# Four gate and up tiles of the FFN made before the attention's last projections, and a new order of loads within a chunk

## The reference, cut to what matters

```python
# B, S, D = 4, 512, 512; 32 heads of 16; FFN width 1376 (padded to 11 tiles of 128)
x = x + attention(layernorm(x))      # qkv with bias, causal, ALiBi bias in the scores, softmax, w_proj, b_proj
h = layernorm(x)
x = x + (silu(h @ w_gate.T) * (h @ w_up.T)) @ w_down.T
```

## Time and profile before

| | |
|---|---|
| median of 3 runs | 911.36 us (910.64 to 912.17) |
| the profiled execution: its time, its span | 909.81 us, 908.1 us |
| TensorE busy (matmuls) | 843.0 us, 93% |
| VectorE busy | 468.9 us, 52% |
| ScalarE busy | 358.1 us, 39% |
| GpSimd busy | 187.8 us, 21% |
| TensorE's mean granted clock | 0.98 of full |
| moved by DMA | 109.33 MB, mean 120 GB/s |

### The profile page before, as it was taken

One profiled execution on the slowest core, in us unless ns is written; L12 is line 12 of the kernel. 1 busy time (PEld: TensorE's weight loads), 2 busy tenths in 40 slices (PEclk: granted clock), 3 DMA queues, 4 the chain that ended last, 5 costly groups with the idle time before them and its releaser, 6 DMA issues. The chain is left out here.

```text
span 908.1 us, 13759 instructions
## 1 busy us (share of the span) xinstructions
PE 843.0 (93%) x5088; PEld 597.8 (66%) x5088; DVE 468.9 (52%) x931; ACT 358.1 (39%) x693; POOL 187.8 (21%) x337
## 2 busy tenths in 40 slices
PE   1998799999999999999998489999999999999998
PEld 1755465656566565656654268887888788878886
DVE  7486766767777676767772353443122322231233
...
GB/s 261 184 238 118 155 133 186 184 137 180 172 222 157 135 179 197 230 128 159 167 200 81 71 298 108 70 1 139 1 1 1 138 1 0 0 94 45 0 0 46
DMA packets 70562, 109.33 MB, mean 120 GB/s; under 512 B 13395, under 2 KB 38662, under 8 KB 70505
## 3 DMA queue, kind: packets, MB, share of 16 engines
...
## 5 line engine op out<-in xcount | busy, mean ns | idle before, releaser
L839 DVE TENSOR_REDUCE bm<-bank 128x3 f32<-128x384 f32 (+1 forms) x384 | 217.5, 593 | 108.2 <-PE bank L1045 107.5
L700 ACT ACTIVATE pt<-bank 128x512 f32<-128x512 f32 (+1 forms) x384 | 196.8, 529 | 175.5 <-PE bank L1067 163.2
L1043 PE MATMUL bank<-k_st,q_st 97*128 97x512 bf16 (+3 forms) x512 | 143.8, 307 | 12.7 <-DMA q_st<-slopes_dram 10.3
L1332 DVE TENSOR_TENSOR gu<-bank,silu 128x512 f32<-128x512 f32 x44 | 30.5, 692 | 219.9 <-issue 130.6
L1143 PE MATMUL bank<-fT_hi,wgu_hi 128*128 128x512 f32 x352 | 138.8, 394 | 5.5 <-DVE wgu_lo L1304 3.5
L1067 PE MATMUL bank<-q_st,k_st 116*128 116x512 bf16 (+3 forms) x512 | 133.1, 303 | 7.3 <-ACT pt L700 6.0
L1143 PE MATMUL bank<-fT_lo,wgu_hi 128*128 128x512 f32 x352 | 138.3, 393 | 0.0
L1143 PE MATMUL bank<-fT_hi,wgu_lo 128*128 128x512 f32 x352 | 137.7, 391 | 0.0
L1045 PE MATMUL bank<-mask_qk,identb 128*128 128x128 bf16 x512 | 107.0, 221 | 0.0
L1043 PEld LDWEIGHTS bank<-k_st,q_st 97*128 97x128 bf16 x512 | 47.4, 98 | 67.9 <-issue 35.6
L1275 ACT ACTIVATE silu<-bank 128x512 f32<-128x512 f32 x44 | 26.3, 598 | 158.2 <-PE bank L1143 158.2
...
## 6 DMA issues: line engine op xcount, KB each, us to landing
...
```

The lines of the kernel that those rows point to most:

```text
L700: act.activation(pt[:, h % PT_RING, COL0[k]:COL0[k] + WIDE[k]], bank[3 + (3 * h + k) % 2][:, 0:WIDE[k]], ACT.Exp, scale=1.0 / HD).then_inc ...
L839: dve.tensor_reduce(bm[:, h % 4, BM_AT[k]:BM_AT[k] + BM_N[k]], bank[k][:, 0:BM_N[k] * P].rearrange("p (n q) -> p n q", q=P), AX.X, ALU.max ...
L1043: pe.matmul(bank[k][:, at:at + n], q_st[0:K_MAX, s, h % 4, t * P:(t + 1) * P], k_st[0:K_MAX, s, h % 4, 0:n], start=True, stop=False)
L1332: dve.tensor_tensor(gu[:, f % 2, :], bank[5 + 2 * (f % 2)][:, :], silu[:, f % 2, :], ALU.mult).then_inc(gu_done, 1)
```

## The change

- Weights: `w_hi` and `w_lo` are now held for the whole program. The attention uses them for w_qkv; from chunk 28 on, when the last q, k, v tile is made, they take the split gate and up weights of FFN tiles 0 to 3 (`EARLY = 4`) and four slots of gated values.
- These weights are loaded in chunks 26 (into the scratch of the parts) and 28 (into `xt`), cast by ScalarE in chunks 28 and 29, split by VectorE in chunks 29 and 30. In chunk 31 the raw weights of tiles 4 and 5 are loaded into `xt`.
- Behind the last weighing TensorE makes tile 0, projection block 2, tiles 1 and 2, block 3, tile 3, for the first batch. ScalarE and VectorE gate them (`gate`, `high`, `gated`).
- In the FFN's first batch `gate_up` runs over tiles 4 to 10; down tiles follow by `DOWN_BEHIND`, down weights are loaded and split on semaphores of their own.
- SyncE: in each chunk the stacks' loads come ahead of the group's load; the store of inverses ahead of Q parts; the store of token tile 2 one chunk later.
- TensorE: token transposes stand behind the weighing (step (0, 1)) and at step (1, 2); the transpose of the maxima one step later.
- ScalarE: copies of transposed tokens behind the head's third exponential; K's second part ahead of it. GpSimd: K's third part ahead of the masks; bias of tile 2 one head later. VectorE: the read of projection tile 2 in the next chunk; the inversion of row sums ahead of the head's last maxima.

```diff
+        w_hi = whole.enter_context(nc.sbuf_tensor("w_hi", [P, KT * 3 * D], F32R))
+        w_lo = whole.enter_context(nc.sbuf_tensor("w_lo", [P, KT * 3 * D], F32R))
+        n = EARLY * 2 * KT * P
+        wgu_e_hi, wgu_e_lo = [w[:, 0:n].rearrange("p (f c k m) -> p f c k m", f=EARLY, c=2, k=KT) for w in (w_hi, w_lo)]
+        gu_hi, gu_lo = [w[:, n:n + EARLY * S].rearrange("p (f s) -> p f s", f=EARLY) for w in (w_hi, w_lo)]
...
+        scratch = sb("scratch", [P, 4 * S])
+        part = scratch[:, 0:3 * S].bitcast(BF16).rearrange("p (c a s) -> p c a s", c=2, a=3)
+        rest = scratch[:, 3 * S:4 * S]
+        wgu_raw = [scratch[:, 2 * S * f:2 * S * (f + 1)].rearrange("p (c k m) -> p c k m", c=2, k=KT) for f in range(2)]
+        wgu_raw += wgu_early
+        silu = scratch[:, 0:2 * S].rearrange("p (f s) -> p f s", f=2)
+        gu = scratch[:, 2 * S:4 * S].rearrange("p (f s) -> p f s", f=2)
...
@@ -532,13 +560,13 @@
             store_parts("Q", 0, 2)
             for c in range(CHUNKS):
                 b, cb = c // CB, c % CB
-                if cb in (1, 3, 7) and loaded_at(c) is not None:
-                    load_group(loaded_at(c))
                 if c + 3 < CHUNKS and cb != 5:
                     load_stacks(c + 3)
                 if cb == 3 and b > 0:
                     load_residual(b - 1, 2)
                     store_tokens(b - 1, 1)
+                if cb in (1, 3, 7) and loaded_at(c) is not None:
+                    load_group(loaded_at(c))
...
                 if cb == 4 and b > 0:
+                    store_tokens(b - 1, 2)
                     store_tokens(b - 1, 3)
                 if cb == 4 and b + 2 <= B:
                     load_tokens(b + 2)
-                if cb == 4 and b == B - 1:
+                if c == CHUNKS - 6:
+                    for s in parts_stored:
+                        sp.wait_ge(s, GROUPS * PARTS_INCS)
+                    for f in range(2):
+                        sp.dma_start(wgu_raw[f], wgu_d[f]).then_inc(raw_in[f], 16)
+                if c == CHUNKS - 4:
                     sp.wait_ge(tile_done, tiles_done("T", B, KT - 1))
+                    for f in range(2, EARLY):
+                        sp.dma_start(wgu_raw[f], wgu_d[f]).then_inc(raw_in[f], 16)
+                if c == CHUNKS - 1:
                     for i in range(2):
-                        sp.dma_start(wgu_early[i], wgu_d[i]).then_inc(early_in[i], 16)
+                        sp.wait_ge(early_lo_done, 2 * (i + 3))
+                        sp.dma_start(wgu_early[i], wgu_d[EARLY + i]).then_inc(early_in[i], 16)
                 if cb == 5:
                     load_group(loaded_at(c))
+                if sums_of(c) is not None:
+                    store_inverses(sums_of(c))
...
-                if cb in (2, 3) and b > 0:
-                    store_tokens(b - 1, 2 * (cb - 2))
-                if sums_of(c) is not None:
-                    store_inverses(sums_of(c))
+                if cb == 2 and b > 0:
+                    store_tokens(b - 1, 0)
...
@@ -637,16 +675,16 @@
                         for kind, mb, g in made(c)[:1]:
                             if kind == "Q":
                                 third_part(kind, mb, g)
-                    clear_future(4 * c + i)
                     if i == 0:
                         for kind, mb, g in made(c - 1)[1:]:
                             if kind == "K":
                                 third_part(kind, mb, g)
+                    clear_future(4 * c + i)
                     if i == 3 and statistics_at(c) is not None:
                         reciprocal_deviation(statistics_at(c))
                     if b > 0 and cb == 1 and i in (0, 2):
                         add_bias(b - 1, i // 2)
-                    if b > 0 and (cb, i) == (3, 2):
+                    if b > 0 and (cb, i) == (3, 3):
...
+            def weight_hi(f, c):
+                act.wait_ge(raw_in[f], 16)
+                act.copy(wgu_e_hi[:, f, c, :, :], wgu_raw[f][:, c, :, :]).then_inc(early_hi_done, 1)
+
+            def gate(f):
+                act.wait_ge(gate_done, f + 1)
+                act.wait_ge(early_lo_done, 2 * EARLY)
+                need(act, gu_done, f - 1)
+                act.activation(silu[:, f % 2, :], bank[GATE_BANK[f % 2]][:, :], ACT.Silu).then_inc(silu_done, 1)
+
+            def high(f):
+                act.wait_ge(gu_done, f + 1)
+                act.copy(gu_hi[:, f, :], gu[:, f % 2, :]).then_inc(gu_hi_done, 1)
...
                     exponential(h, 0)
-                    if tokens_at(c, i) is not None and i == 0:
-                        transposed_hi(*tokens_at(c, i))
                     if i == 3:
                         for tile in made(c)[:1]:
                             if tile[0] == "Q":
                                 second_part(*tile)
                     exponential(h, 1)
-                    if tokens_at(c, i) is not None and i == 1:
-                        transposed_hi(*tokens_at(c, i))
+                    if i == 0:
+                        for tile in made(c - 1)[1:]:
+                            if tile[0] == "K":
+                                second_part(*tile)
                     if highs(c, i) is not None:
                         attention_hi(*highs(c, i))
                     exponential(h, 2)
+                    if tokens_at(c, i) is not None:
+                        transposed_hi(*tokens_at(c, i))
...
+                    if c in (CHUNKS - 4, CHUNKS - 3):
+                        weight_hi(2 * (c - CHUNKS + 4) + i // 2, i % 2)
             attention_hi(*highs(CHUNKS, 0))
             copy_pv(CHUNKS - 1)
+            gate(0)
+            high(0)
             for i in range(HALVES):
                 attention_hi(LAST, i)
+            for f in range(1, EARLY):
+                gate(f)
+                high(f)
...
+            def weight_lo(f, c):
+                dve.wait_ge(early_hi_done, 2 * f + c + 1)
+                dve.tensor_tensor(wgu_e_lo[:, f, c, :, :], wgu_raw[f][:, c, :, :], wgu_e_hi[:, f, c, :, :].bitcast(F32),
+                                  ALU.subtract).then_inc(early_lo_done, 1)
+
+            def gated(f):
+                dve.wait_ge(silu_done, f + 1)
+                dve.wait_ge(up_done, f + 1)
+                need(dve, gu_hi_done, f - 1)
+                dve.tensor_tensor(gu[:, f % 2, :], bank[GATE_BANK[f % 2] + 1][:, :], silu[:, f % 2, :],
+                                  ALU.mult).then_inc(gu_done, 1)
+                dve.wait_ge(gu_hi_done, f + 1)
+                dve.tensor_tensor(gu_lo[:, f, :], gu[:, f % 2, :], gu_hi[:, f, :].bitcast(F32),
+                                  ALU.subtract).then_inc(gu_lo_done, 1)
...
@@ -920,11 +992,17 @@
                     scored(0)
                     if i == 3:
                         for tile in made(c)[:1]:
-                            read_tile(*tile)
+                            if (tile[0], tile[2]) != ("P", 2):
+                                read_tile(*tile)
                     scored(1)
+                    if i == 3 and sums_of(c) is not None:
+                        invert_row_sums(sums_of(c))
                     if i == 1 and c + 1 < CHUNKS:
                         copy_maxima(c + 1)
                     if i == 0:
+                        for tile in made(c - 1)[:1]:
+                            if (tile[0], tile[2]) == ("P", 2):
+                                read_tile(*tile)
...
+                    if c in (CHUNKS - 3, CHUNKS - 2):
+                        weight_lo(2 * (c - CHUNKS + 3) + i // 2, i % 2)
 
             for i in range(HALVES):
                 for a, half in lows(CHUNKS, i):
                     attention_lo(a, half)
+            gated(0)
...
+            gated(1)
+            gated(2)
             for t in range(TT):
                 add_projection(B - 1, t)
+            gated(3)
...
@@ -1107,23 +1189,44 @@
             for c in range(CHUNKS):
                 for i in range(4):
                     h = 4 * c + i
-                    if i == 0 and tokens_at(c, 0) is not None:
-                        transpose_tokens(*tokens_at(c, 0))
                     for k in range(3):
                         scores(h + AHEAD, k)
+                        if (i, k) == (1, 1) and c + 1 < CHUNKS:
+                            transpose_maxima(c + 1)
+                        if (i, k) == (1, 2) and tokens_at(c, 1) is not None:
+                            transpose_tokens(*tokens_at(c, 1))
                         shifted_scores(h, k)
                         if i > 0 and k < 2:
                             between(c, 8 * (i - 1) + 4 * k, 8 * (i - 1) + 4 * k + 4)
                         if (i, k) == (0, 1) and c > 0:
                             weigh_values(c - 1, (0, 1, 3, 2))
-                        if (i, k) == (1, 0) and c + 1 < CHUNKS:
-                            transpose_maxima(c + 1)
-                        if (i, k) == (1, 0) and tokens_at(c, 1) is not None:
-                            transpose_tokens(*tokens_at(c, 1))
```

(53 more changed lines are left out.)

143 lines of the change are left out of this document (81 added, 62 removed).

## The result

The changed kernel takes 880.09 us (median of 4 runs, 878.74 to 883.48), the kernel before 911.0 us beside it: ratio 0.9665, 95% interval 0.9635 to 0.9694. The forecast was 889.4 us, range 881 to 902. The direction and the two places of the gain (loop and seam) were right, the size was not: the gain is 31 us where 22.0 were forecast. The profiled execution has a span of 877.0 us against 908.1, so its account adds up to 31.1 us.

What follows compares the result with a forecast made beforehand. TensorE, busy 93% of the span, was the bound: fill its pauses or restore its clock. 10.6 + 3.5 + 15.9 - 2.5 - 1.5 - 4.0 = 22.0 us, from 911.4 to 889.4 us, range 881 to 902.

Steps and rivals of the forecast that it cites:

- The FFN's blocks have nothing to gain but by having less work in them: From 528 us on the chain of waits is matmuls alone, so no gain was forecast from faster matmuls.
- Waits that come back elsewhere: In the attention loop, filling a pause brings other waits nearer: a quarter of 15.9 us, 4.0 us, charged.
- the 1.5 for the bank: In eight chunks the second token transpose stands close ahead of the projection into the same bank: 1.5 us charged.
- Stack loads: In the loop, earlier loads and K parts save 7.3 of 8.3 us of TensorE's waits and 3.0 of clock.
- Token transposes: In the loop, moving them behind the weighing saves 3.0 of 3.4 us of waits for tokens and the bank.
- Tile 2's read: In the loop, VectorE's read of projection tile 2 no longer holds up the maxima: 1.7 of 2.2 us.
- Maxima's transpose: In the loop, placing it one step later on TensorE saves 0.9 of 1.8 us.
- Inverses ahead: In chunk 30, earlier inversion of row sums removes the wait before the last weighing and its clock loss: 3.5 us.
- The splits: In chunks 28 to 30, splitting early weights on ScalarE and VectorE costs 2.5 us, bounds 0 and 4.9.
- The seam: Between attention and FFN, four gate and up tiles fill TensorE's 8.73 us wait: gain 10.6 us.
- rival C: Attention groups come late behind stack loads in six chunks, up to 26 us, 916 us: slower 2%, in part 2%.
- Rival B: At FFN entry the first down weight comes 2.5 us late, perhaps 1.7 more: 892 to 894 us; chance 6%.

Runs made afterwards that it cites:

- loop orders alone: The kernel before with all reorderings inside the loop, the inversion included, and no tile moved early: 895.38 us, ratio 0.9827.
- places alone: The kernel before with early tiles' weights and two slots of gated values placed in `w_hi` and `w_lo`, orders unchanged: 906.96 us, ratio 0.9949.
- the seam alone: The changed kernel with every order within a chunk put back; early tiles, their split and the weights' places stay: 897.04 us, ratio 0.9833.
- four slots: The kernel before with four slots of gated values instead of two and the wait for them loosened: 910.82 us, ratio 0.9978.

## Why the prediction was wrong, step by step

The sum was 10.6 + 3.5 + 15.9 - 2.5 - 1.5 - 4.0 = 22.0 us, and 31.1 came between the two traces. Of the 9.1 us between them, 3.8 are a term that wasn't in the sum, the FFN's blocks; 2.1 the loop orders with the last weighing (16.0 instead of 13.9); 1.1 the splits (-1.4 instead of -2.5); 0.7 the seam; and 1.3 arose ahead of chunk 1 and are not the change's (with rounding). The 16.0 are the 14.0 up to the transpose for chunk 29 and the 2.0 that the loop orders alone gain from there to the end of the last weighing (42.26 us before, 40.22 with them).

- **"The FFN's blocks have nothing to gain but by having less work in them": failed, 3.8 us.** This is the largest miss; without it the time would have stood inside the range. The same matmuls became faster by place alone: 3.7 us in three blocks with places alone, 1.3 more in block 0 where only the gated values moved. The earlier trace rows shows 2.80 us per down tile and 5.49 per 24 gate and up matmuls, 0.233 and 0.229 us for each of one shape, so there was a trace of it: two prices for one shape. The forecast took them as given.
- **Waits that come back elsewhere, charged 4.0: about right, though guessed.** Up to the transpose for chunk 29, 3.6 us came back. A quarter of the gross wasn't read from a row. The gross itself was 17.3 us there (13.9 of waits, 3.4 of clock) where the forecast has 15.9, and the 1.5 for the bank didn't arise. The forecast's list of waits leaves out the second largest, 4.3 us in eleven waits for exponentials from 60 to 490 us; it is these that stay and grow. The loop orders alone gave 15.7 us (14.9 by spans), where the forecast's terms for them are 15.9 + 3.5 - 1.5 - 4.0 = 13.9.
- **Stack loads, 7.3 of 8.3 us and 3.0 of clock: right in mechanism.** The waits are gone, as are the two low windows; the gain is 3.6 us into chunk 5, 2.6 into chunk 7. The run with K's parts late gives +3.6 there, and that with stacks last +2.5 into 5.
- **Token transposes, 3.0 of 3.4, less 1.5 for the bank: the net about right (2.0, where 1.5 was forecast), the charge not.** The interval with the first of them lost 3.9 with clock when put back. No matmul waits for the bank in the new place; what the old one saves is 1.2 us of waiting for the transposed maxima, in one interval.
- **Tile 2's read, 1.7: not shown.** Put back, it gave back no wait in chunks 12, 20, 28. **Maxima's transpose, 0.9: right.** Put back, the waits at it grow from 1.9 to 2.8 us. In the changed kernel they are 1.9 in spite of it, as in the earlier trace rows, because the two into chunks 3 and 4 are longer than in the old order (0.72 us each instead of 0.46).
- **Inverses ahead, 3.5 us at the last weighing: the size came (3.46), but not by this step.** With the inversion late, that stretch is 0.24 us longer, not 3.5. The old order's own wait isn't fixed either: 1.94 us in the profiled execution, 0.86 with four slots, none with the places alone. What the earlier inversion gives is in the intervals into 11 and 17, where without it VectorE stands for the group's load.
- **The splits, -2.5: 1.1 too much, and by another path.** The two intervals lost 2.8 us, but the loop orders alone lose 1.4 of them; the same comparison in the old order (the seam alone against the kernel before) gives 1.4 to 1.5. The path is ScalarE's issue and casts ahead of an exponential, where the forecast named VectorE's maxima.
- **The seam, 10.6: measured 11.3** from the last weighing's end to the end of the block, of which about 1 us is the faster matmuls. The pause was 4.06 where 4.75 was forecast: its end of block took 0.5 us (520.69 to 521.20) instead of 1.29. Half clock behind it came as forecast.
- **Groups late behind the stacks (rival C): not in the changed kernel.** Between 60 and 475 us VectorE stands at none of its 28 divisions (L920) for a load, where it waited 3.5 us in three before, and in chunk 9 it starts the division 8.34 us after the group's issue with no wait, where the earlier trace rows has 8.13 and 1.48 of waiting. The group is now issued 2.8 us before the chunk's maxima transpose instead of 0.9. The rival's 3.0 us for 768 KB ahead of a group was not seen: with the stacks ahead, a group issued 0.09 us before the transpose was waited for by nobody, with the group ahead and 0.85 us before it VectorE waited 1.48. In small it did happen in seven of the nine other kernels of the new order, 0.1 to 1.3 us in one or two chunks each. The Trainium skill ("DMA: Bandwidth & Descriptors", "Queues, rings and completion order") says that on each DMA engine descriptors are taken in ring order. No run here measures that order; what these traces show is only that the groups were not later for the stacks ahead of them. Rival B (the FFN starved) didn't occur: there is no pause after 522.59.

The time lay 0.9 us under the range, whose low end was set with "all gains and no charge" but without a term for matmuls that get faster.
